# An adaLN, state-space and quantised-FFN kernel on one core: the per-iteration order of small matmuls, gate projections and transposes is rearranged

## The reference, cut to what matters

```python
proj = einsum('bld,pd->blp', h, in_proj_w)       # gate 4096, x 4096, B 1024, C 1024, dt 64
xBC  = silu(causal conv of 4 taps over [x, B, C])
dt_p = softplus(dt + dt_bias); dA = exp(-exp(A_log) * dt_p)
state = state * dA_t + (dt_p * x)_t outer B_t ;  y_t = state . C_t     # 64 heads of 64, 8 groups
y    = y + x * D ; per group of 512: y * rsqrt(mean(y^2) + eps) * norm_weight
out  = (y * silu(gate)) @ out_proj_w.T
```

## Time and profile before

| | |
|---|---|
| Time, median of 3 runs | 3525.2 us (3523.05 to 3527.17) |
| The profiled execution: its own time, its span | 3524.74 us, 3523.0 us |
| Mean granted TensorE clock over the span | 0.993 of full speed |
| TensorE matmul busy | 3457.4 us, 98% |
| TensorE weight loads busy | 2871.1 us, 81% |
| VectorE busy | 3060.7 us, 87% |
| ScalarE busy | 1452.9 us, 41% |
| GpSimd busy | 476.2 us, 14% |
| DMA moved | 477.75 MB, mean 136 GB/s |

### The profile page before, as it was taken

One profiled execution on the slowest core, in us unless ns is written; L12 is line 12 of the kernel. 1 busy time (PEld: TensorE's weight loads), 2 busy tenths in 40 slices (PEclk: granted clock), 3 DMA queues, 4 the chain that ended last, 5 costly groups with the idle time before them and its releaser, 6 DMA issues. The chain is left out here.

```text
span 3523.0 us, 58511 instructions
## 1 busy us (share of the span) xinstructions
PE 3457.4 (98%) x19725; PEld 2871.1 (81%) x19725; DVE 3060.7 (87%) x4827; ACT 1452.9 (41%) x2194; POOL 476.2 (14%) x334
## 2 busy tenths in 40 slices
PE   6699999999999999999999999999999999999999
PEld 4488888888888888888888888888888888888888
DVE  5599999999999999999999999999999999998443
ACT  3444444444444444444444444444444444343111
POOL 4201111011111011111011111011111011111333
PEclk9799999999999999999999999999999999999999
DMA  7623335333533354333533363334433352224331
GB/s 254 252 102 110 117 148 184 114 131 110 200 131 119 113 191 134 116 131 119 196 131 111 115 215 120 112 131 166 144 131 120 112 197 83 84 95 145 91 92 57
DMA packets 216067, 477.75 MB, mean 136 GB/s; under 512 B 39082, under 2 KB 84554, under 8 KB 206434
## 3 DMA queue, kind: packets, MB, share of 16 engines
q1 hardware_dynamic: 212356, 476.30, 38.8%
q0 software_dynamic: 304, 0.82, 0.1%
q10 hardware_dynamic: 3376, 0.26, 0.1%
HBM read 316.32 MB, written 161.01 MB: 135 GB/s over the span
## 5 line engine op out<-in xcount | busy, mean ns | idle before, releaser
L838 PE MATMUL p_cv<-ht,wt 128*128 128x512 f32 x5376 | 1298.8, 394 | 5.7 <-DMA ht<-h_d 5.7
L838 PEld LDWEIGHTS p_cv<-ht,wt 128*128 128x128 f32 x5376 | 1000.9, 188 | 231.4 <-issue 16.9
L934 PE MATMUL bank<-wot,gy 128*128 128x512 f32 x3072 | 737.7, 396 | 0.0
L934 PEld LDWEIGHTS bank<-wot,gy 128*128 128x128 f32 x3072 | 567.2, 188 | 128.7 <-issue 11.0
L1076 DVE SCALAR_TENSOR_TENSOR xc<-p_cv,cvw,xc 128x496 f32<-128x496 f32 (+2 forms) x768 | 544.5, 716 | 27.8 <-ACT xc L987 9.6
L838 PE MATMUL bank<-ht,wt 128*128 128x512 f32 x2304 | 562.0, 393 | 0.0
L987 ACT ACTIVATE xc<-p_cv,cvb,cvw 128x512 f32<-128x512 f32 x256 | 199.8, 781 | 863.2 <-PE p_cv L838 863.2
L838 PEld LDWEIGHTS bank<-ht,wt 128*128 128x128 f32 x2304 | 427.7, 188 | 87.9
L813 POOL TENSOR_TENSOR r<-rv,neg_half 128x4 f32<-128x4 f32 x64 | 89.7, 1402 | 2418.8 <-DVE rv L1164 2418.8
L1098 DVE TENSOR_TENSOR m<-cbm,y 128x1024 f32<-128x1024 f32 x256 | 301.6, 1220 | 7.8
L977 ACT ACTIVATE gy<-z 128x512 fp32r<-128x512 f32 x256 | 162.0, 633 | 331.7 <-DVE z L1138 331.7
(11 more groups left out here) (187 smaller groups left out, 3565.2 us busy)
## 6 DMA issues: line engine op xcount, KB each, us to landing
ht<-h_d SPq DMA_DIRECT2D x64, 2048.0 KB, 7.8
acc<-acc_d SPq DMA_DIRECT2D x64, 1024.0 KB, 7.0
acc_d<-acc SPq DMA_DIRECT2D x64, 1024.0 KB, 4.3
wt_d<-wnext SPq DMA_DIRECT2D x112, 512.0 KB, 3.1
wt<-wt_d SPq DMA_DIRECT2D x70, 512.0 KB, 8.3
stage<-in_L_attn_in_proj_w SPq DMA_DIRECT2D x94, 256.0 KB, 2.7
h_d<-ht_out SPq DMA_DIRECT2D x8, 2048.0 KB, 8.2
wot<-wt_d SPq DMA_DIRECT2D x28, 512.0 KB, 6.0
```

Of the source, the lines that this page charges most:

```text
L838: ins = pe.matmul(pb[:, :], wt[:, n, l, k, :], ht[:, rr, k, :], start=(q == 0 and k == 0), stop=(q == 2 and k == KC - 1))
L934: ins = pe.matmul(bank[OUT[t]][:, :], gy[:, c, l, t * P:(t + 1) * P], wot[:, rr, c, :], start=(c == 0 and q == 0), stop=(c == CT - 1 and q ...
```

## The change

TensorE's new order is P0 to P5, CB, N0, N1, SEG, P6, P7, P8, X0, X1, X2, X3, S0, S1, P9, S2, S3, O with SSQ. The four X tiles now go to four banks (3, 4, 5, 7) and N0 and N1 to banks 3 and 4. So the X transposes wait, beside silu, for both exp (which read banks 5 and 7) and for the low parts of the next weights (banks 3 and 4), but no longer for `dtx` of an earlier tile. ScalarE makes the two copies of the next weights before the exps. VectorE makes `cbm` before the conv of slice 5, then, after the conv, the low parts of the next weights, then all four `m` tiles, then all four `dtx` tiles. SP's and GpSimd's code is the same. No operation is added or left out.

```diff
--- before.py
+++ after.py
@@ -610,7 +610,7 @@
         warm = sb("warm", [P, 1])
 
         bank = sh.p_cv + [ctx.enter_context(nc.psum_tensor(f"bank{n}", [P, 512], F32)) for n in range(2, 8)]
-        XT, SEG, CB, YB, OUT, SSQ, NEXT = (3, 4), (5, 7), 6, (6, 7), (2, 3, 4, 5), 6, (5, 1)
+        XT, SEG, CB, YB, OUT, SSQ, NEXT = (3, 4, 5, 7), (5, 7), 6, (6, 7), (2, 3, 4, 5), 6, (3, 4)
 
 
         s_stage = [sem(f"s2_stage{n}") for n in range(NSTAGE)]
@@ -842,7 +842,7 @@
                     def turn_x(t):
 
                         for c in range(CT):
-                            ins = pe.transpose(bank[XT[t % 2]][:, c * P:(c + 1) * P], xc[:, 2 + c, t * P:(t + 1) * P], sh.ident[:, :])
+                            ins = pe.transpose(bank[XT[t]][:, c * P:(c + 1) * P], xc[:, 2 + c, t * P:(t + 1) * P], sh.ident[:, :])
                         ins.then_inc(s_xt, 1)
 
                     def scan(c):
@@ -867,44 +867,39 @@
                             pe.wait_ge(s_conv, NCV * it + n - 2)
                         project(n)
 
+                    pe.wait_ge(s_silu, NCV * it + 2)
+                    pe.wait_ge(s_rv, it + 1)
+                    pe.wait_ge(s_y, CT * it + CT)
+                    for t in range(TT):
+                        ins = pe.matmul(bank[CB][:, t * P:(t + 1) * P], xc[:, 0, t * P:(t + 1) * P], xc[:, 1, t * P:(t + 1) * P],
+                                        start=True, stop=True)
+                    ins.then_inc(s_cb, 1)
+
+                    pe.wait_ge(s_acc, TT * it + TT)
+                    for u in range(2 if prepare else 0):
+                        pe.wait_ge(s_raw[u], 16 * it + 16)
+                        for k in range(KC):
+                            ins = pe.transpose(bank[NEXT[u]][:, k * P:(k + 1) * P], stage[u][:, k * P:(k + 1) * P], sh.ident[:, :])
+                        ins.then_inc(s_nps, 1)
+
                     pe.wait_ge(s_segr, 2 * it + 4)
                     pe.wait_ge(s_acc, TT * it + TT)
-                    pe.wait_ge(s_y, CT * it + CT)
                     for q in range(SEGB):
                         for half in range(2):
                             ins = pe.matmul(bank[SEG[q]][:, :], sh.mask_gtr[:, :],
                                             segr[:, half, q * 2 * HG:(q + 1) * 2 * HG, :].rearrange("p h l -> p (h l)"),
                                             start=(half == 0), stop=(half == 1))
                         ins.then_inc(s_seg, 1)
-                    pe.wait_ge(s_conv, NCV * it + 4)
-                    project(NCV)
-
-                    pe.wait_ge(s_silu, NCV * it + 2)
-                    pe.wait_ge(s_rv, it + 1)
-                    for t in range(TT):
-                        ins = pe.matmul(bank[CB][:, t * P:(t + 1) * P], xc[:, 0, t * P:(t + 1) * P], xc[:, 1, t * P:(t + 1) * P],
-                                        start=True, stop=True)
-                    ins.then_inc(s_cb, 1)
-
-                    for c in (1, 2):
+                    for c in range(CT - 1):
                         pe.wait_ge(s_conv, NCV * it + 4 + c)
                         project(NCV + c)
-                        for t in (2 * c - 2, 2 * c - 1):
-                            if c == 1:
-                                pe.wait_ge(s_silu, NCV * it + NCV)
-                            else:
-                                pe.wait_ge(s_dtx, TT * it + t - 1)
-                            turn_x(t)
-
-                    for u in range(2 if prepare else 0):
-                        pe.wait_ge(s_raw[u], 16 * it + 16)
-                        if u == 0:
-                            pe.wait_ge(s_exp, SEGB * it + 1)
-                        else:
-                            pe.wait_ge(s_z, CT * it + CT + 2)
-                        for k in range(KC):
-                            ins = pe.transpose(bank[NEXT[u]][:, k * P:(k + 1) * P], stage[u][:, k * P:(k + 1) * P], sh.ident[:, :])
-                        ins.then_inc(s_nps, 1)
+
+                    pe.wait_ge(s_silu, NCV * it + NCV)
+                    pe.wait_ge(s_exp, SEGB * it + SEGB)
+                    if prepare:
+                        pe.wait_ge(s_nlo, 2 * it + 2)
+                    for t in range(TT):
+                        turn_x(t)
                     pe.wait_ge(s_cbm, it + 1)
                     scan(0)
                     pe.wait_ge(s_exp, SEGB * it + SEGB)
@@ -988,6 +983,10 @@
                                        scale=cvw[:, n, TAPS - 1:TAPS]).then_inc(s_tap, 1)
                         if 0 < n < NCV - 1:
                             silu(n - 1)
+                    for u in range(2 if prepare else 0):
+                        act.wait_ge(s_nps, 2 * it + u + 1)
+                        act.wait_ge(s_nst, 32 * it + 32)
+                        act.activation(wnext[:, u, 0, :], bank[NEXT[u]][:, :], ACT.Copy).then_inc(s_nhi, 1)
                     for q in range(SEGB):
                         act.wait_ge(s_seg, SEGB * it + SEGB + q + 1)
                         act.activation(decay[:, 2 * q:2 * q + 2, :, :].rearrange("p t h l -> p (t h l)"),
@@ -997,11 +996,6 @@
                     gate(0)
                     gate(1)
                     gate(2)
-
-                    for u in range(2 if prepare else 0):
-                        act.wait_ge(s_nps, 2 * it + u + 1)
-                        act.wait_ge(s_nst, 32 * it + 32)
-                        act.activation(wnext[:, u, 0, :], bank[NEXT[u]][:, :], ACT.Copy).then_inc(s_nhi, 1)
                     high(0)
                     high(1)
                     gate(3)
@@ -1068,7 +1062,15 @@
                     dve.wait_ge(s_adt, 4 * it + 3)
                     dve.tensor_tensor(adts[:, 1, :], adt_v, adts[:, 0, :].bitcast(F32), ALU.subtract).then_inc(s_adt, 1)
 
+                    def spread_cb():
+
+                        dve.wait_ge(s_cb, it + 1)
+                        dve.tensor_tensor(cbm[:, :, :], bank[CB][:, :].rearrange("p (t n) -> p t n", t=TT),
+                                          sh.mask_cb[:, :].unsqueeze(1).to_broadcast([P, TT, P]), ALU.mult).then_inc(s_cbm, 1)
+
                     for n in range(NCV):
+                        if n == NCV - 1:
+                            spread_cb()
                         dve.wait_ge(s_tap, NCV * it + n + 1)
                         for k in range(1, TAPS):
                             src = bank[PROJ_BANK[n]][:, :].rearrange("p (b l) -> p b l", l=L)[:, :, 0:L - k]
@@ -1088,10 +1090,6 @@
                             pair(3, ld, 0)
                             find_here(0)
 
-                    dve.wait_ge(s_cb, it + 1)
-                    dve.tensor_tensor(cbm[:, :, :], bank[CB][:, :].rearrange("p (t n) -> p t n", t=TT),
-                                      sh.mask_cb[:, :].unsqueeze(1).to_broadcast([P, TT, P]), ALU.mult).then_inc(s_cbm, 1)
-
                     def scan_matrix(t):
 
                         dve.wait_ge(s_exp, SEGB * it + t // 2 + 1)
@@ -1103,24 +1101,19 @@
 
                         dve.wait_ge(s_xt, TT * it + t + 1)
                         dve.tensor_tensor(dtx[:, t, :].rearrange("p (h c) -> p h c", h=HG),
-                                          bank[XT[t % 2]][:, :].rearrange("p (h c) -> p h c", h=HG),
+                                          bank[XT[t]][:, :].rearrange("p (h c) -> p h c", h=HG),
                                           sh.dt[:, ds(TT * j + t, 1), ds(HG * g, HG)].rearrange("p o h -> p (o h)").unsqueeze(2).to_broadcast([P, HG, HP]),
                                           ALU.mult).then_inc(s_dtx, 1)
 
                     dve.wait_ge(s_cbm, it + 1)
-                    scan_matrix(0)
-                    scan_matrix(1)
-                    times_dt(0)
-                    times_dt(1)
-                    scan_matrix(2)
-                    scan_matrix(3)
-                    times_dt(2)
-                    times_dt(3)
-
                     for u in range(2 if prepare else 0):
                         dve.wait_ge(s_nhi, 2 * it + u + 1)
                         dve.tensor_tensor(wnext[:, u, 1, :], bank[NEXT[u]][:, :], wnext[:, u, 0, :].bitcast(F32),
                                           ALU.subtract).then_inc(s_nlo, 1)
+                    for t in range(TT):
+                        scan_matrix(t)
+                    for t in range(TT):
+                        times_dt(t)
                     def low(c):
 
                         dve.wait_ge(s_uhi, CT * it + c + 1)
```

## The result

The changed kernel takes 3554.98 us (median of 4, 3553.56 to 3557.14); the kernel before, run beside it, 3525.47. The ratio is 1.0083, with a 95% interval from 1.0071 to 1.0095: slower by 29.5 us. The profiled execution took 3555.91 us, 31.2 more than that of before.

A forecast was written before the change was run, and what follows sets the result against it. TensorE's own stream was taken to bound the kernel. A 0.88 us stall less 0.07 of stream, 56 x 0.81 + 8 x 0.25 = 47.4 us, gave 3573 us; bounds 3566 and 3581, range widened to 3540 and 3605.

The forecast's parts named there:

- (a): In S0: VectorE's four dtx end after S0 wants them; 3573 us, 3560 to 3590, chance 0.74.
- the widening to 3540: Whole kernel: range widened to 3540 and 3605 for 8 in 10, taking in a stall of a third.
- the 0.83 us: VectorE ahead of dtx0: it starts 0.83 us after X0, as dtx2 did after X2 before.
- My lower bound, 0.72: Ahead of dtx0: 0.72 (ScalarE's reply time to N0) in place of 0.83, giving 0.70 us per iteration.
- The stream: TensorE from P5's end to S0: 12.78 us instead of 12.85, a gain of 0.07 us per iteration.
- The last group: Its 8 iterations without N: the four dtx end at 3176.71 against 3176.46, 0.25 us lost in each.
- The covers: ScalarE and VectorE ahead of X0: 3 to 5 us of cover, so X0 starts on time at 10.94.
- the margin behind a turn: N0 in the first iteration after a turn: raw rows land 1.4 us before it starts, so no stall.
- (b): In S0: dtx hides and only the run of projections shows; 3512 to 3521 us, chance 0.09.
- (c): In S0: stream gain and short stall cancel, or S0 absorbs the wait; within 7 us of 3525, chance 0.06.
- (d): At X0: late because silu 5, exps or low parts are late; 3629 us at 1 us per iteration, chance 0.07.
- (e): In the run of transposes: TensorE's clock falls once per iteration, 2.4 us each time; 3707 us, chance 0.04.

The follow-up runs named there:

- The rotated tiles: The changed kernel with the tiles turned, multiplied and scanned in the order 1, 2, 3, 0: 3564.49 us, ratio 1.0114.
- the kernel with N behind X: The changed kernel with N0 and N1, their copies and low parts put back behind X3, into banks 1 and 2: 3517.56 us, ratio 0.9978.
- CB ahead alone: The kernel before with only CB moved ahead of SEG and cbm ahead of conv 5: 3519.30 us, ratio 0.9985.
- the kernel with half the cover: The changed kernel with N0 still ahead of SEG and N1 put back behind X3 in bank 2: 3532.27 us, ratio 1.0022.

## Why the prediction was right, and where its size was off

The mechanism was the forecast one, its size 0.6 of it. The four signs named for it came: TensorE waits for dtx in all 64 iterations, for 0.73 us in the middle of S0; the iteration is longer (48.54 us, 48.8 forecast); VectorE idles 1.00 us ahead of dtx0; P6 to P8 take 8.17 us. One of the signs of being wrong came as well: dtx0 starts well before 0.8 us after X0.

The time lies below the lower bound of the working (3566) and below the range of the case (a) that was chosen (3560 to 3590). Only the widening to 3540 holds it, and that was an allowance for the unknown, not knowledge of the term that was off.

Term by term, in us from P5's end, for an iteration with N:

| Step of the prediction | forecast | measured |
|---|---|---|
| X0 starts | 10.94 | 10.87 |
| dtx0 starts after X0 | 0.83 | 0.63 |
| first dtx to the end of the fourth | 2.49 | 2.53 |
| end of dtx to P9 | 1.30 | 1.30 |
| P9 starts (before: 14.75) | 15.56 | 15.33 |
| iteration longer by | 0.81 | 0.53 |
| iteration of the last group longer by | 0.25 | 0.03 |

- **The mis-sized term is the 0.83 us.** "dtx2 started 0.83 after X2's start ... with VectorE idle for it": I took the distance for the reply time of TensorE and the tag of the wait at its word. 0.2 us of it was a register operation behind the wait, which dtx2 has and dtx0 has not. The rotated tiles put it back, and the time rose by 9.5 us. My lower bound, 0.72, was above the truth as well. This term carries 0.20 of the 0.28 us by which the iteration was overestimated.
- **The stream** of TensorE was underrated: X0 came 0.07 earlier than summed, and P9 itself took 2.95 (1565.05 to S2's start at 1568.00) instead of 2.99, of which nothing was forecast. From P5's end to P9 the kernel with N behind X gains 0.14 us over before, not 0.07; CB ahead alone is worth 5.4 us.
- **The last group** lost 0.03 instead of 0.25: the same 0.2 again. The sum 56 x 0.53 + 8 x 0.03 = 29.9 us stands against 29.5 measured (31.2 between the two profiled executions).
- **The covers held.** cbm started 1.09 us after CB and conv 5 1.70 after P5's end, both as worked out. ScalarE's copies began at 1.61 (forecast 1.59), silu 5 ended at 7.57 (7.5). Its timeline in the changed kernel has no new table load: only the two around the exps, which the kernel before has too (the first is in the earlier trace rows):

```profile
1551.33 1.09 ACT L989 ACTIVATE wnext<-bank 128x512 fp32r<-128x512 f32 x2 [0.63 <-PE bank L882]
1552.44 1.28 ACT L992 ACT_TABLE_LOAD   x1
1553.73 1.09 ACT L992 ACTIVATE y<-bank 128x512 f32<-128x512 f32 x2
1554.84 1.28 ACT L964 ACT_TABLE_LOAD   x1
1556.13 1.16 ACT L964 ACTIVATE xc<-xc 128x512 f32<-128x512 f32 x2
```

  The four m tiles ended at 10.5, ahead of the first X tile. Neither the matmuls nor the weight loads of N (L882) have any idle time ahead of them in the whole run, so the margin behind a turn was enough. It was some 0.9 us there and not 1.4: two loads were issued from 575.48 with P5's end at 578.73.
- **The rivals.** (b), dtx hidden and only the stream's gain left, did not come for this change; it is what the kernel with N behind X shows: 3517.56, inside the 3512 to 3521 given for it. (c) did not come: the loss of 29.5 us is outside its 7. (d) did not come: nothing was late at X0. (e) did not come: the window has a clock of 1.00 with sixteen transposes in a row. Its one argument, that the run is longer, was weak, since the kernel before has sixteen in a row too (X2, X3, N0, N1); only the stall is new. By the rule of the Trainium skill (TensorE: Matmul & The Clock Gate, Part 4: PE-mode transpose) such a run might have lowered it; no run here shows that.

What stays open: what makes the four scans in one run 0.16 us shorter and the groups of transposes cheaper by some hundredths when they follow each other. It was seen in the timelines, not taken apart.

## What to carry to other kernels

On an engine that is busy throughout, a short piece of unrelated work can be a cover for another engine: N0 and N1 hid the last dtx tiles, and P9 hid y. Before moving such a piece, look for the chain on the other engine that ran under it and subtract; the loss is just what is then uncovered. Follow the in-order DMA queue as well: a wait that is moved late there holds up every load behind it. And when a reply time is read off a row, look whether register operations stand between the wait and the instruction.

## What the runs showed of the hardware that was not expected

- A register operation of 151 ns, by the code that of an operand's offset, ran only when the wait ahead of it was over: 0.85 instead of 0.63 us from the first transpose to the first product, 9.5 us in 64 iterations. In the waits it appears as idle time ended by TensorE.
- The waits on the row of matmuls understate a stall of TensorE; those on the row of the weight loads hold it. 64 stalls of some 0.7 us in S0 and S1 (2.63 against 1.90) stand as 10.1 us on the first and as 48.5 us on the second. In the kernel with half the cover, stalls of 0.29 us (2.19 against 1.90) are missing from the first in the 56 iterations with N; the second has 22.9 us. Of these, 5.8 are taken to be the last group's, as in the kernel with N behind X, which leaves an estimate of 0.31 for each of the 56. The distance from start to start shows both as well.
- After 4.02 us of idle the granted clock was 0.62 in the next 3.53 us and 1.7 us were lost over two projections, on top of the gap.
